# GpSimd's first state of the second graph moved, one cast of ScalarE moved, and the last layer's gates on 480 of 512 columns

## The reference, cut to what matters

```python
A = (adj != 0)
h = x
for l in range(5):
    m = einsum('bnd,de->bne', h, weight[l])
    agg = einsum('bij,bid->bjd', A, m)
    gi = agg @ w_ih.T + b_ih;  gh = h @ w_hh.T + b_hh      # each split in r, z, n
    r = sigmoid(i_r + h_r);  z = sigmoid(i_z + h_z)
    n = tanh(i_n + r * h_n)
    h = (1 - z) * n + z * h
x = layernorm(x + h * mask)
x = layernorm(x + graph_convolutions_on_nodes_0_to_24(x))  # five groups of nodes, two layers each
```

## Time and profile before

| | us |
|---|---|
| median of 3 runs | 497.56 (497.54 to 498.7) |
| profiled execution, its time | 498.51 |
| its span | 496.8 |
| TensorE busy | 484.0 (97%) |
| VectorE, ScalarE, GpSimd busy | 377.7, 297.3, 321.1 |

### The profile page before, as it was taken

The page is one execution under the profiler, slowest core; times in us unless marked ns, Lnnn a source line. Parts: engine busy times, 40 slices in busy tenths (PEclk is TensorE's granted clock), DMA queues, the critical chain, the costliest instruction groups (busy, mean ns, idle before and its releaser), DMA issues.

```text
span 496.8 us, 7148 instructions
## 1 busy us (share of the span) xinstructions
PE 484.0 (97%) x2305; PEld 229.7 (46%) x2305; DVE 377.7 (76%) x711; ACT 297.3 (60%) x524; POOL 321.1 (65%) x318
## 2 busy tenths in 40 slices
PE   7899999999999999999999999999999999999995
PEld 5344444444444444434444444444444444564564
DVE  3867967686867588999689877878868896445796
ACT  4456555655555656666666675565655667645555
POOL 3554785648784688875789548569886655224466
PEclk9999999999999999999999999999999999999999
DMA  8769252666525537345847476324543233212313
GB/s 273 233 144 188 56 148 44 159 139 170 122 55 143 131 86 187 77 99 120 183 97 168 103 210 168 67 43 80 111 86 82 48 65 76 55 36 44 80 45 85
DMA packets 133732, 55.97 MB, mean 113 GB/s; under 512 B 97257, under 2 KB 125374, under 8 KB 133694
## 3 DMA queue, kind: packets, MB, share of 16 engines
q1 hardware_dynamic: 108316, 32.39, 32.0%
q10 hardware_dynamic: 25378, 23.12, 15.1%
HBM read 27.70 MB, written 4.19 MB: 64 GB/s over the span
## 4 chain that ended last, share of the span: by engine, by line
PE 79%; DVE 11%; DMA 3%; issue 2%; ACT 2%; POOL 2%; SPq 1%; POOLq 0%; ACTq 0%; DVEq 0%
PE pA L762 23%; PE pR L769 6%; PE pR L767 6%; PE pR L768 6%; PE pZ L768 6%; PE pZ L769 6%; PE pZ L767 6%; PE pHN L767 3%; PE pHN L768 3%; PE pHN L769 3%; PE pIN L767 3%; PE pIN L769 3%; PE pIN L768 3%; DVE T L1359 2%; DMA AS<-in_adj_dram 1%
## 5 line engine op out<-in xcount | busy, mean ns | idle before, releaser
L522 POOL TENSOR_TENSOR HT<-H,HT 128x512 f16<-128x512 f32 x76 | 91.3, 1201 | 105.3 <-ACT HT L1131 105.1
L762 PE MATMUL pA<-A,NAT 128*128 128x512 fp8e4 x640 | 151.4, 379 | 1.5 <-DVE A L1348 1.1
L511 POOL TENSOR_TENSOR ZH<-Z,H 128x512 f32<-128x512 f32 x80 | 102.3, 1279 | 29.9 <-ACT Z L1144 28.1
L1359 DVE SCALAR_TENSOR_TENSOR T<-pHN,BHN,R 128x512 f32<-128x512 f32 x80 | 59.9, 749 | 67.1 <-ACT R L1137 66.8
L1148 ACT ACTIVATE pIN<-T,COLS 128x512 f32<-128x512 f32 x80 | 55.4, 692 | 79.0 <-DVE T L1363 78.9
L762 PEld LDWEIGHTS pA<-A,NAT 128*128 128x128 f16 x640 | 62.2, 98 | 77.1 <-issue 2.0
L1131 ACT ACTIVATE HT<-H 128x512 f16<-128x512 f32 x76 | 47.8, 629 | 65.8 <-DVE H L1372 65.6
L1368 DVE SCALAR_TENSOR_TENSOR pIN<-Z,pIN 128x512 f32<-128x512 f32 x80 | 55.1, 689 | 22.7 <-ACT pIN L1148 22.6
L1137 ACT ACTIVATE R<-pR,BRZ 128x512 f32<-128x512 f32 x80 | 54.4, 680 | 23.1 <-PE pR L769 22.8
L1354 DVE TENSOR_TENSOR AG<-pA,AG 128x512 f16<-128x512 f32 x80 | 54.7, 684 | 6.9 <-ACT AG L1127 6.8
L1372 DVE TENSOR_TENSOR H<-ZH,pIN 128x512 f32<-128x512 f32 x80 | 54.9, 687 | 4.3 <-POOL ZH L511 1.6
(11 more groups left out here) (282 smaller groups left out, 832.9 us busy)
## 6 DMA issues: line engine op xcount, KB each, us to landing
AS<-in_adj_dram ACTq DMA_DIRECT2D x13, 1024.0 KB, 6.1
XR<-in_x_dram ACTq DMA_DIRECT2D x16, 256.0 KB, 2.9
XS<-in_x_dram ACTq DMA_DIRECT2D x13, 256.0 KB, 3.1
out_dram<-Y SPq DMA_DIRECT2D x16, 192.0 KB, 2.3
AS<-in_adj_dram SPq DMA_DIRECT2D x2, 1024.0 KB, 8.6
AS<-in_adj_dram SPq DMA_DIRECT2D x4, 256.0 KB, 5.4
NAT<-HT SPq DMA_TRANSPOSE x64, 3.1
XS<-in_x_dram SPq DMA_DIRECT2D x3, 256.0 KB, 7.7
```

Source lines behind the costliest of these rows:

```text
L511: g_.tensor_tensor(ZH[:, :], Z[:, :], H[:, b, :], ALU.mult).then_inc(zh_p, 1)
L522: g_.tensor_tensor(HT[:, b, 1, :], H[:, b, :], HT[:, b, 0, :], ALU.subtract).then_inc(h_lo, 1)
L762: last = mm(pA2[:, k % 2, :], NAT[:, k % 2, h, i, :], A8[:, b, i, :], start=(h == 0 and i == 0), stop=(h == 1 and i == NI - 1))
L1359: v.scalar_tensor_tensor(out=T[:, :], in0=pHN[:, :], scalar=BHN[:, 0:1], in1=R[:, :], op0=ALU.add, op1=ALU.mult).then_inc(t_v, 1)
```

## The change

It has three parts. In GpSimd's list, `first_state(1)` moves from ahead of `kept_share(0)` to behind `natural_lo(2)`. In ScalarE's list, `natural_hi(2)` moves from behind `aggregated_hi(1)` to ahead of `new_gate(0)`. And in steps 76 to 79 the gates, `Z * H`, the candidate and the new state work on columns 32 to 511 (`COLS_OF[k]`); the aggregation and its two f16 parts keep 512.

```diff
+COLS_OF = [slice(S if t >= K - Q else 0, N) for t in range(K)]
...
-                g_.tensor_tensor(ZH[:, :], Z[:, :], H[:, b, :], ALU.mult).then_inc(zh_p, 1)
+                cs = COLS_OF[k]
+                g_.tensor_tensor(ZH[:, cs], Z[:, cs], H[:, b, cs], ALU.mult).then_inc(zh_p, 1)
...
             natural_lo(0)
             first_state(0)
             natural_lo(1)
-            first_state(1)
             kept_share(0)
             natural_lo(2)
+            first_state(1)
             state_lo(0)
...
-                ht = [HT[:, b, h, :] for h in range(2)]
+                cs = COLS_OF[k]
+                ht = [HT[:, b, h, cs] for h in range(2)]
...
-                split_product(pHN, WH[:, 0, 2, :], WH[:, 1, 2, :], ht[0], ht[1], True, True)
+                split_product(pHN[:, cs], WH[:, 0, 2, :], WH[:, 1, 2, :], ht[0], ht[1], True, True)
...
-                ag = [AG[:, k % 2, h, :] for h in range(2)]
+                ag = [AG[:, k % 2, h, cs] for h in range(2)]
...
             load_a(3)
+            natural_hi(2)
             new_gate(0)
             aggregated_hi(1)
-            natural_hi(2)
```

More of the change, by code:

```diff
@@ L766, in split_product @@
             def split_product(bank, w_hi, w_lo, v_hi, v_lo, start, stop):
-                mm(bank[:, :], w_hi, v_hi, start=start, stop=False)
-                mm(bank[:, :], w_hi, v_lo, start=False, stop=False)
-                return mm(bank[:, :], w_lo, v_hi, start=False, stop=stop)
+                mm(bank, w_hi, v_hi, start=start, stop=False)
+                mm(bank, w_hi, v_lo, start=False, stop=False)
+                return mm(bank, w_lo, v_hi, start=False, stop=stop)
             def gates_of_state(k, between=lambda: None):
                 b = GRAPH[k]
-                ht = [HT[:, b, h, :] for h in range(2)]
+                cs = COLS_OF[k]
+                ht = [HT[:, b, h, cs] for h in range(2)]
                 if k < 2:
@@ L780, in gates_of_state @@
                     pe.wait_ge(t_v, k)
-                split_product(pHN, WH[:, 0, 2, :], WH[:, 1, 2, :], ht[0], ht[1], True, True)
+                split_product(pHN[:, cs], WH[:, 0, 2, :], WH[:, 1, 2, :], ht[0], ht[1], True, True)
                 if k > 0:
                     pe.wait_ge(sig_r, k)
-                split_product(pR, WH[:, 0, 0, :], WH[:, 1, 0, :], ht[0], ht[1], True, False)
+                split_product(pR[:, cs], WH[:, 0, 0, :], WH[:, 1, 0, :], ht[0], ht[1], True, False)
                 between()
@@ L787, in gates_of_state @@
                     pe.wait_ge(sig_z, k)
-                split_product(pZ, WH[:, 0, 1, :], WH[:, 1, 1, :], ht[0], ht[1], True, False)
+                split_product(pZ[:, cs], WH[:, 0, 1, :], WH[:, 1, 1, :], ht[0], ht[1], True, False)
             def first_gates_of_state():
@@ L804, in first_gates_of_state @@
                 first_messages()
-                split_product(pZ, WH[:, 0, 1, :], WH[:, 1, 1, :], hi, lo, True, False)
+                split_product(pZ[:, :], WH[:, 0, 1, :], WH[:, 1, 1, :], hi, lo, True, False)
             def gates_of_messages(k, between=lambda: None):
-                l = LAYER[k]
-                ag = [AG[:, k % 2, h, :] for h in range(2)]
+                l, cs = LAYER[k], COLS_OF[k]
+                ag = [AG[:, k % 2, h, cs] for h in range(2)]
                 wc = [[WC[:, l, h, g, :] for g in range(3)] for h in range(2)]
@@ L813, in gates_of_messages @@
                 pe.wait_ge(ag_lo, k + 1)
-                split_product(pR, wc[0][0], wc[1][0], ag[0], ag[1], False, True).then_inc(r_mm, 1)
-                split_product(pZ, wc[0][1], wc[1][1], ag[0], ag[1], False, True).then_inc(z_mm, 1)
+                split_product(pR[:, cs], wc[0][0], wc[1][0], ag[0], ag[1], False, True).then_inc(r_mm, 1)
+                split_product(pZ[:, cs], wc[0][1], wc[1][1], ag[0], ag[1], False, True).then_inc(z_mm, 1)
                 between()
@@ L819, in gates_of_messages @@
                     pe.wait_ge(h_v, k)
-                split_product(pIN, wc[0][2], wc[1][2], ag[0], ag[1], True, True).then_inc(in_mm, 1)
+                split_product(pIN[:, cs], wc[0][2], wc[1][2], ag[0], ag[1], True, True).then_inc(in_mm, 1)
             def early_aggregate():
@@ L1136, in reset_gate @@
                     act.wait_ge(t_v, k)
-                fn(R[:, :], pR[:, :], ACT.Sigmoid, bias=BRZ[:, 0:1], scale=UNSCALE).then_inc(sig_r, 1)
+                cs = COLS_OF[k]
+                fn(R[:, cs], pR[:, cs], ACT.Sigmoid, bias=BRZ[:, 0:1], scale=UNSCALE).then_inc(sig_r, 1)
             def update_gate(k):
@@ L1143, in update_gate @@
                     act.wait_ge(e_v, k)
-                fn(Z[:, :], pZ[:, :], ACT.Sigmoid, bias=BRZ[:, 1:2], scale=UNSCALE).then_inc(sig_z, 1)
+                cs = COLS_OF[k]
+                fn(Z[:, cs], pZ[:, cs], ACT.Sigmoid, bias=BRZ[:, 1:2], scale=UNSCALE).then_inc(sig_z, 1)
             def new_gate(k):
                 act.wait_ge(u_v, k + 1)
-                fn(pIN[:, :], T[:, :], ACT.Tanh, bias=BI[:, 2:3], scale=UNSCALE).then_inc(n_a, 1)
+                cs = COLS_OF[k]
+                fn(pIN[:, cs], T[:, cs], ACT.Tanh, bias=BI[:, 2:3], scale=UNSCALE).then_inc(n_a, 1)
             def masked(b):
@@ L1357, in candidate @@
             def candidate(k):
+                cs = COLS_OF[k]
                 dve.wait_ge(sig_r, k + 1)
-                v.scalar_tensor_tensor(out=T[:, :], in0=pHN[:, :], scalar=BHN[:, 0:1], in1=R[:, :],
+                v.scalar_tensor_tensor(out=T[:, cs], in0=pHN[:, cs], scalar=BHN[:, 0:1], in1=R[:, cs],
                                        op0=ALU.add, op1=ALU.mult).then_inc(t_v, 1)
@@ L1362, in candidate @@
                 dve.wait_ge(in_mm, k + 1)
-                v.tensor_tensor(T[:, :], pIN[:, :], T[:, :], ALU.add).then_inc(u_v, 1)
+                v.tensor_tensor(T[:, cs], pIN[:, cs], T[:, cs], ALU.add).then_inc(u_v, 1)
             def new_state(k):
+                cs = COLS_OF[k]
                 dve.wait_ge(n_a, k + 1)
-                v.scalar_tensor_tensor(out=pIN[:, :], in0=Z[:, :], scalar=1.0, in1=pIN[:, :],
+                v.scalar_tensor_tensor(out=pIN[:, cs], in0=Z[:, cs], scalar=1.0, in1=pIN[:, cs],
                                        op0=ALU.subtract, op1=ALU.mult).then_inc(e_v, 1)
@@ L1371, in new_state @@
                 dve.wait_ge(zh_p, k + 1)
-                v.tensor_tensor(H[:, GRAPH[k], :], ZH[:, :], pIN[:, :], ALU.subtract).then_inc(h_v, 1)
+                v.tensor_tensor(H[:, GRAPH[k], cs], ZH[:, cs], pIN[:, cs], ALU.subtract).then_inc(h_v, 1)
             def early_lo():
```

## The result

The changed kernel took 496.13 us (median of 6 runs, 495.61 to 496.29), the one before 497.79 (6 runs, 497.54 to 499.21): a ratio of 0.996, 95% interval 0.9946 to 0.9973, or 1.66 us less by the medians. By the means of the six it is 2.0 less, and the interval of the ratio is 1.3 to 2.7 us. I had forecast 495.2, that is 2.34 less. The profiled execution went from a span of 496.8 to 494.4, which is the 2.3 of the forecast nearly to the digit. That agreement is misleading, and most of what follows is about why the profiles differ by 2.4 and the medians by 1.66.

A forecast was written before the change was run, and what follows sets the result against it. TensorE's matmuls were taken as the time from 31 to 483 us, with the start worth one to one. Front 1.82 plus tail 0.52 made 2.34 off the median 497.56, so 495.2 us; range 494.3 to 496.5.

The forecast's parts named there:

- The bound: TensorE's matmuls are the time between 31 and 483 us; starting step 4's aggregation earlier moves the end one to one.
- The front, 1.82 us: Start of the kernel up to aggregation 4: without `first_state(1)` beside them, graph 1's casts finish sooner, `T` of step 0 1.82 us earlier.
- The second part, nothing: Graph 2's high half ahead of the first tanh: neither gives nor takes, by itself worth nothing on the chain.
- The transpose among loads: Rival: step 2's transpose lands at 23.75 or later, so TensorE's list sets step 4; total -1.5, 496.0 us; chance 0.11.
- The tail, 0.52 us: Steps 76 to 79 with 480 columns: narrower matmuls and elementwise work, less three waits, save 0.52 us.
- The first wait: At `early_aggregate`, 466.32: TensorE arrives 0.36 us early and waits 0.36 for the transpose of step 79.
- The step to `early_back`: Second wait in the tail, at 473.85, behind `early_state` on VectorE: shorter elementwise work and an earlier sigmoid give 0.16 us.
- The slower case: Rival: `natural_hi(2)` waits for a late `x` of graph 2 and delays the tanh; slower by over 1.5 us; chance 0.04.
- The dead front: Rival: graph 1's second cast stands behind `Z * H`, or casts were slow otherwise; only the tail remains, 497.0 us; chance 0.11.
- The whole tail: Rival: no wait holds in the 480-column steps; 2.9 us less in all, 494.6 us; chance 0.05.

The follow-up runs named there:

- the run with the tail's order: The changed kernel with `early_aggregate` and `back(E0)` moved behind the first three message matmuls of step 77; ratio 0.9959 to the kernel before.

## Why the prediction was right, and where it was off

**The bound.** Right. The value of the front is one to one: over all fourteen profiles the way from aggregation 4 to the end is the same within 0.13 us for one tail, but for the one slow transpose.

**The front, 1.82 us.** The mechanism is right and shown: the casts stand still while GpSimd works, and an instruction that nobody waits for brings the loss back. The term is mis-sized. I took the casts' 3.12 as what the kernel before does, from one profile whose time of 498.51 I had noted to lie 0.95 above the median, and then moved that 0.95 over unchanged. It was not offset: most of it was this very term. Against the 15.5 from first cast to aggregation 4 after the change, the kernel before and the kernels with its GpSimd order have 16.40, 16.42, 16.44, 16.77 and 17.34: a gain of 0.9 in three of five, 1.3 and 1.8 in the others, 1.15 in the mean. The first and second part together measured 0.95 us (interval 0.35 to 1.5), which leaves the 1.82 out. Four of the kernel before's six times in the comparison of the result lie in its lower group, and so does their median; against that outcome 0.9 and the tail's 0.67 are 1.6, and 1.66 was measured. Against the mean outcome the sum is 1.8, and by the means it was 2.0. I named the race for the new order (the second cast must begin before `Z * H`, 0.69 us to spare), but did not ask whether the old order had one too, with 0.27 us and 0.05 us between the starts.

**The second part, nothing.** Right as a number for that part alone (1.0004), wrong as a statement. I checked only whether a later low half would make its transpose late, which it does not (22.43 with the old list). I did not follow `first_state(1)`, which the first part puts behind that low half, into the casts of graph 2. Without the second part the first loses over half of its gain: 16.06 from first cast to aggregation 4, beside 15.49 with the second part. The transpose among loads landed in 4.8 us in the profile after, and in 5.9 in another run, where it cost 0.35.

**The tail, 0.52 us.** Measured 0.65 to 0.67. The first wait is as worked out: `early_aggregate` did not move (435.47 and 435.44 from aggregation 4), TensorE waited 0.34. The step to `early_back` was put at 0.16 and measured 0.34 (443.00 to 442.66). What I missed is a wait that stood behind the one I named: `back(E0)` needs the state of step 76, which in the profile before ended at 466.60 and let it start at 466.65, and after at 464.73 and 464.79. That state is made by narrower operations and came 0.14 earlier. The two lines of the kernel before:

```profile
465.91 0.69 DVE L1372 TENSOR_TENSOR H<-ZH,pIN 128x512 f32<-128x512 f32 x1
...
466.65 0.66 PE L868 MATMUL pF<-IDF,H 128*128 128x128 f32 x4
```

Before, `back(E0)` began 0.33 behind `early_aggregate`, after 0.23. So the sigmoid of step 77 gained 0.17, from 0.03 at `early_aggregate`, this 0.10 and the 0.04 from three matmuls, which was all that I had counted. The rest of the elementwise list gave 0.17 (0.12 counted), the remaining matmuls 0.25 (0.24 counted, from 442.66 to the last candidate at 451.60), and the operations behind it the last 0.08.

**The rivals.** The slower case did not come: `x` of graph 2 was in time. In the run with the tail's order its high half began only at 15.31, though, 0.3 short of the 15.6 from which it delays the tanh. The dead front, with the second cast behind `Z * H`, did not come in any of the eight profiles without an instruction in the freed place. The whole tail did not come; the wait for the transpose is real.

**What was luck.** 496.13 lies above the 494.8 to 495.7 that I gave the forecast by itself. It lies in the whole range because I had opened that upwards for a late transpose of step 2 and for spread between runs, and not for a smaller front, which is what came. And that the span fell by 2.4, as forecast, is no support for the 1.82: it is measured from the same profile that the term was read from, the one with the dearest outcome.

## What to carry to other kernels

Before pricing the removal of a hold-up between two engines, look at how close their starts are in the profile: with 0.05 to 0.3 us between them, one profile shows one outcome of a race. The gain is the difference to each outcome, weighed by how often it comes, and only further profiles and the spread of the times show that. When an instruction moves behind another, follow it through every stretch in which the other can be late, since it may only hold up the next pair. And measure parts from a landmark that does not move (here from the first cast, and from aggregation 4): the whole times differ by more than the parts do.

## What the runs showed that I had not expected

- Held up, GpSimd's 1.15 us instruction took 1.47 to 1.60 and its 1.27 one 1.52 to 1.72; so an operation's own record holds its waiting for the other engine, and no line of waits shows it.
- In the kernel after, TensorE's first transposes of `x` took 0.42 us each and not 0.27, and followed each other by 0.21 and not 0.11, at a printed clock of 1.00 in both profiles. The first cast, 13.60, stood behind a `lo` part at 12.99, while its load was there by 13.3, so this may have cost the changed kernel's own front up to 0.3 us; why they were slow the profile does not say.
- A DMA transpose took 3.0 us alone, 4.8 and 5.9 among the first loads, and 9.51 once in the middle of a run, where it cost the span 0.3.
